# Two-layer graph network on one core: the MLP's products as column tiles between the edge groups, and first nodes read four at a time

## What is computed

```python
h = jnp.maximum(_layernorm(x), 0.0)
agg = segment_sum(edge_attr_64, dst) / jnp.maximum(counts, 1.0)[:, None]
x = x + (relu(concat([agg, h], 1) @ W1 + b1) @ W2 + b2)      # W1: 320 x 512, W2: 512 x 256
h = jnp.maximum(_layernorm(x), 0.0)
neigh = segment_sum(h[src], dst) / jnp.maximum(deg, 1.0)[:, None]
x = x + h @ w_self.T + b_self + neigh @ w_neigh.T
```

## Time and profile before

| | |
|---|---|
| median of 3 runs | 1132.64 us (1132.23 to 1134.74) |
| the profiled execution, its own time | 1135.44 us |
| its span (first to last instruction) | 1133.5 us |
| TensorE busy | 1072.6 us, 95% |
| VectorE busy | 787.8 us, 70% |
| ScalarE busy | 494.5 us, 44% |
| GpSimd busy | 521.7 us, 46% |
| mean granted TensorE clock | 0.985 of full speed |

### The profile page before, as it was taken

How to read it: one execution, slowest core, us unless ns; L and a number is a source line. 1 busy time by engine, 2 the same in 40 slices (tenths; PEclk the granted TensorE clock), 3 DMA queues, 4 the chain that set the end, 5 groups by cost and what they waited for, 6 DMA issues and landing times.

```text
span 1133.5 us, 29643 instructions
## 1 busy us (share of the span) xinstructions
PE 1072.6 (95%) x11380; PEld 792.0 (70%) x11380; DVE 787.8 (70%) x1849; ACT 494.5 (44%) x957; POOL 521.7 (46%) x502
## 2 busy tenths in 40 slices
PE   3689999999999999699999999999999999999998
PEld 2667777777777777467767777677677777776765
DVE  6778878887883667766766676766676767666762
ACT  4455646342212546444444444444444444444441
POOL 3011111110002664377576766774767676677520
PEclk9899999999999999699999999999999999999999
DMA  8776655555562221133233233332333333333210
GB/s 259 226 212 202 198 162 166 153 162 161 173 198 93 77 61 44 51 98 104 79 108 96 86 99 95 95 101 71 112 94 102 91 98 94 94 97 99 79 44 19
DMA packets 72618, 131.93 MB, mean 116 GB/s; under 512 B 12414, under 2 KB 32594, under 8 KB 72492
## 3 DMA queue, kind: packets, MB, share of 16 engines
q1 hardware_dynamic: 51820, 75.25, 21.7%
q0 software_dynamic: 20672, 55.00, 16.9%
HBM read 117.25 MB, written 12.95 MB: 115 GB/s over the span
## 4 chain that ended last, share of the span: by engine, by line
PE 87%; DVE 6%; DVEq 2%; ACT 2%; issue 2%; DMA 1%; ACTq 0%; SPq 0%
PE bank L1216 35%; PE couples L1209 10%; PE couples L1039 9%; PE bank L1235 7%; PE bank L984 7%; PE bank L996 6%; PE bank L978 2%; PE bank L1247 2%; PE bank L1227 2%; PE couples L1044 2%; PE couples L949 1%; DVE oreg L1647 1%; PE couples L984 1%; DVE oreg L1396 1%; DVEq L1511 1%
## 5 line engine op out<-in xcount | busy, mean ns | idle before, releaser
L1216 PE MATMUL bank<-hreg,areg 128*128 128x512 f16 x1862 | 457.0, 383 | 0.0
L629 POOL DMA_INDIRECT wide<-h_table,aggn x332 | 354.6, 1068 | 193.8 <-PE couples L1209 95.2
L847 ACT ACTIVATE areg<-couples 128x784 bf16<-128x784 f32 x304 | 250.3, 824 | 351.0 <-PE couples L1209 342.1
L1216 PEld LDWEIGHTS bank<-hreg,areg 128*128 128x128 bf16 x1862 | 240.4, 144 | 95.1 <-issue 1.6
L1647 DVE TENSOR_TENSOR hids<-iota,kreg 128x1024 bf16<-128x1024 f16 (+1 forms) x304 | 177.8, 626 | 110.0 <-PE couples L1209 108.9
L1647 DVE TENSOR_TENSOR oreg<-iota,kreg 128x1024 bf16<-128x1024 f16 (+1 forms) x304 | 177.7, 626 | 24.5 <-PE couples L1209 23.4
L1039 PEld LDWEIGHTS couples<-oreg,kreg 128*64 128x64 f32 x3232 | 117.2, 142 | 64.7 <-issue 63.6
L1039 PE MATMUL couples<-oreg,kreg 128*64 128x48 f32 x3232 | 138.5, 230 | 21.3 <-DVE oreg L1396 16.7
L597 POOL TENSOR_TENSOR xr<-xr,b2bc 128x512 f32 x25 | 33.9, 1356 | 221.0 <-ACT h0buf L719 221.0
L1396 DVE TENSOR_TENSOR oreg<-iota,wide 128x384 f32<-128x384 f32 x202 | 121.5, 602 | 4.4 <-issue 1.3
L996 PE MATMUL bank<-wide,hids 128*128 128x256 f32 x400 | 104.4, 398 | 0.0
(11 more groups left out here) (176 smaller groups left out, 1102.2 us busy)
## 6 DMA issues: line engine op xcount, KB each, us to landing
kreg<-in_edge_attr_dram SPq DMA_DIRECT2D x202, 256.0 KB, 2.8
h_table<-hreg SPq DMA_DIRECT2D x25, 256.0 KB, 2.2
xr<-in_x_dram SPq DMA_DIRECT2D x6, 1024.0 KB, 7.6
wide<-h_table,aggn POOLq DMA_INDIRECT x332
out_dram<-hbuf SPq DMA_DIRECT2D x38, 128.0 KB, 1.9
out_dram<-h0buf SPq DMA_DIRECT2D x10, 128.0 KB
wide<-in_L_gnn_W_dram SPq DMA_DIRECT2D x2, 512.0 KB, 8.5
hids<-h_table,aggn POOLq DMA_INDIRECT x64
```

What stands on the lines that cost most here:

```text
L629: pool.indirect_dma_start(near_rows(n % RING, w), None, table, bass.IndirectOffsetOnAxis(ap=nearsrc[:, k:k + 1], axis=0)).then_inc(s_rows[ ...
L847: act.activation(step.rearrange("p (a k) -> p a k", a=2), cpl[s % 2][:, :, 0:BC * KEYS], ACT.Copy).then_inc(s_adj, 1)
L1216: ins = pe.matmul(bank[4 + par], adj[:, par, :, h], htab[:, h, :], start=(h == 0), stop=(h == TN - 1))
```

## The change

- In the spans, `hidden` and `outer` are called with `beside=True`. Each product is then two, one for each half of its stationary columns (`halves_of`), written to the two halves of PSUM's partitions: column tiles of 64, as the groups' products are.
- `w1a` is no longer used as row tiles there: each piece multiplies all 128 rows of `w1a` (which holds the 64 rows of weights twice) by all 128 rows of `aggn[:, q, :]`. The half of `aggn` that DVE does not write for this q must be zero, so GpSimd clears `aggn` at the start, ahead of `acc`. The product with `w1a` for q = 1 moves into the piece of q = 1.
- PE's hardware loop over spans 2 to 5 is written out.
- The table `base` is clamped to 0..N-1 as it is written, and DVE reads the first nodes of groups g to g+3 in one load when g is a multiple of 4, without the range assertion; the three other groups use registers that are already filled.

```diff
+            pool.memset(aggn[:, :, :], 0.0)
             pool.memset(acc[:, :], 0.0).then_inc(s_const, 1)
...
+            def halves_of(beside):
+
+                return (slice(0, FE), slice(FE, P)) if beside else (slice(0, P),)
+
+            def hidden(i, k, b, q, own=0, beside=False):
...
-                    for e in qs:
-                        pe.matmul(hidden_bank(e, k, own)[:, b * NM:(b + 1) * NM], w1a[e * FE:(e + 1) * FE, cols],
-                                  aggn[e * FE:(e + 1) * FE, e, :], start=True, stop=False)
+                    if not beside:
+                        for e in qs:
+                            pe.matmul(hidden_bank(e, k, own)[:, b * NM:(b + 1) * NM], w1a[e * FE:(e + 1) * FE, at:at + P],
+                                      aggn[e * FE:(e + 1) * FE, e, :], start=True, stop=False)
...
+                if beside:
+
+                    for m in halves_of(beside):
+                        pe.matmul(into[m, :], w1a[:, at + m.start:at + m.stop], aggn[:, q, :], start=True, stop=False)
                 for h in range(DH):
-                    ins = pe.matmul(hidden_bank(q, k, own)[:, b * NM:(b + 1) * NM], w1b[:, h, cols],
-                                    h0T[:, bass.ds(2 * u, 2), h, :], start=False, stop=(h == DH - 1))
+                    for m in halves_of(beside):
+                        ins = pe.matmul(into[m, :], w1b[:, h, at + m.start:at + m.stop],
+                                        h0T[:, bass.ds(2 * u, 2), h, :], start=False, stop=(h == DH - 1))
...
-                    ins = pe.matmul(bank[6 + q][:, t * D:(t + 1) * D], hids[:, q, b, t * P:(t + 1) * P], w2s[:, b, :],
-                                    start=(b == 0), stop=(b == HB - 1))
+                    for m in halves_of(beside):
+                        ins = pe.matmul(bank[6 + q][m, t * D:(t + 1) * D], hids[:, q, b, t * P + m.start:t * P + m.stop],
+                                        w2s[:, b, :], start=(b == 0), stop=(b == HB - 1))
...
-                            part(i, *which)
+                            part(i, *which, beside=True)
...
-                loop(pe, lambda k: span(k, k - 1), 2, XPARTS)
+                for k in range(2, XPARTS):
+                    span(k, k - 1)
...
-            dve.tensor_copy(base[0:1, :], bank[6][0:1, 0:G]).then_inc(s_base, 1)
+            dve.tensor_scalar(base[0:1, :], bank[6][0:1, 0:G], 0.0, float(N - 1), ALU.max, ALU.min).then_inc(s_base, 1)
...
-                    return dve.value_load(base[0:1, bass.ds(SLOTS * i + q, 1)], min_val=0, max_val=N - 1)
+                    g = SLOTS * i + q
+                    if g % STARTS == 0:
+                        _, found = nc.values_load_multi_w_load_instructions(
+                            base[0:1, g:min(g + STARTS, G)], engines=[dve.engine], min_val=0, max_val=N - 1,
+                            skip_runtime_bounds_check_because="they are clamped as they are written")
+                        starts.update({g + n: v for n, v in enumerate(found)})
+                    return starts.pop(g)
```

More of the change, by code:

```diff
@@ L64, in gnn_kernel @@
     LAG = PARTS - 1
+    STARTS = 4
     H0 = 2, 2 + U
```

7 lines of the change are left out of this document (4 added, 3 removed).

## The result

The kernel before took 1133.67 us (median of 6 runs, 1132.23 to 1134.74), the changed one 1124.00 us (6 runs, 1119.82 to 1125.81). The ratio is 0.9902, 95% interval 0.9886 to 0.9918: 9.7 us less, where 27.4 were forecast. The time lies above the range.

A forecast was written before the change was run, and what follows sets the result against it. PE sets the pace from 72 to 343 us, DVE following closest. 29.4 - 1.5 + 1.0 - 0.5 - 1.0 = 27.4 us saved; 1132.64 - 27.4 = 1105.2, stated as 1106, range 1101 to 1117.

The forecast's parts named there:

- The mechanism on PE: Outer and hidden pieces, 72 to 343 us: tile-shape changes go, saving 17.9 and 11.5 us, together 29.4 of PE's 271.
- The rival of the exposed weight loads: PE's pieces: 560 instruction pairs each show 0.06 us of weight loading, 4.2 us slower, 1137; chance 0.05.
- that of the gaps that stay: PE's pieces: the 0.32 us gaps are not the tile's change and remain, 6.4 us slower, about 1139; chance 0.03.
- the charge for DVE: DVE's dense places in the spans: PE waits 0.3 us in each of five spans, 1.5 us lost.
- the dense place: DVE from the means at 208.04 to 219.97 us: 11.6 us busy against PE's 11.0 over the same eight groups.
- DVE's waits for PE: 72 to 343 us: without waits of 26.1 and 8.4 us DVE needs 236.5, PE 241.6; DVE fits, 5 us to spare.
- my second case, DVE takes over: Edge-group stretch: half of DVE's 34.5 us of waits stay as order; gain 17.5 us, time about 1116; chance 0.17.
- Edge rows: Edge loads behind three parts of x in the units: a wait of some 0.1 us and more each, charged 1.0 us.
- the stages after the last group, counted as shifted whole: Stages after 343 us: neither shortened nor lengthened by the change, only moved earlier.
- Reads: DVE's reads of first nodes, before 72 us: 27 reads fewer at 0.05 us each, 1.0 us gained.
- Start: Kernel start: clearing aggn ahead of acc holds DVE's index cast and shifts the whole start, 0.5 us lost.

The follow-up runs named there:

- the covered branch: Changed kernel with the first two hidden parts behind the spans moved ahead of the branch ending PE's group code: ratio 0.9871 to the kernel before.
- the best kernel: Changed kernel plus hidden pieces ahead of the branch, late x in four pieces, b2 added by TensorE for the seven units: 1109.81 us, 0.9762; again 1108.03, 0.9760.
- the kernel without column tiles: Kernel before with reads by four, covered branch, x in pieces and b2 on TensorE, loop over spans kept: 1126.78 us, 0.9919.

## Why the prediction was wrong

**The mechanism on PE and its size were right.** Outer piece and group went from 1.780 to 1.468 us: 0.31 us instead of 0.32, 56 x 0.312 = 17.5. A hidden pair went from 2.394 + 1.780 to 2 x 1.900 us: 0.37 instead of 0.41, 28 x 0.374 = 10.5. Together 28.0 us off PE, forecast 29.4. The rival of the exposed weight loads is out (1.47 and 1.90 us, halves 7 ns apart), as is that of the gaps that stay. The Trainium skill ("TensorE: Matmul & The Clock Gate", Part 3, The mechanism) has a list by which a weight load overlaps with matmuls in flight only where the rows differ, though the paragraph above it also lets a load into a background buffer go ahead. Here tiles with the same 128 rows follow each other at 0.216 us a pair, the time of streaming alone, so the measurement decides against the list's rule.

**The step that failed is the charge for DVE: 1.5 us, measured 12.3.** From the table: outer pieces stall for 89.7 - 79.3 = 10.4 us where the kernel before had 99.7 - 54 x 1.780 = 3.6, so 6.8; plain groups 29.1 - 23.6 = 5.5. I had found the dense place and priced it by its sum over eight groups (11.6 us of DVE against 11.0 of PE), at 0.3 us for each of five spans. PE does not wait for the sum but for single one-hots, three buffers ahead at most. In that very stretch of the kernel before DVE takes 3.3 us from one one-hot to the next (their ends, 211.31 and 214.57), where PE was to need 1.47:

```profile
211.35 0.22 DVE L1403 TENSOR_SCALAR deg<-areg 64x128 f32<-64x128 f32 x1
211.64 0.94 DVE L1405 RECIPROCAL deg<-deg 64x128 f32<-64x128 f32 x1
212.60 0.42 DVE L1392 TENSOR_TENSOR areg<-areg,couples 64x48 f32 x2
213.05 1.52 DVE L1396 TENSOR_TENSOR oreg<-iota,wide 128x384 f32<-128x384 f32 x1
```

Two things come together in it. One is GpSimd's addition of b2 (212.88 to 214.15): the one-hot took 1.52 us instead of 0.56, and I counted it without asking why. The trace of before had ten one-hots of over 0.8 us, 7.1 us of stretching in them, and a mean of 0.60 us for a one-hot. Leaving the addition out gives the stretch 6.6 us after (7.9 but for the lower clock) and 2.5 before, so 4.1 to 5.4 of the 12.3 us are the collisions'. The Trainium skill ("SBUF — State Buffer", SBUF: two separate sides) describes a port pair that VectorE and GpSimd hold one at a time for a whole instruction; the rows agree in the main (a one-hot begun at 207.89 under an addition that ends at 208.89 ends at 209.30, 0.41 us later, of the 0.56 that it takes alone). The other, the larger part, is what is left: DVE's own work, dense around the inverses and means, found by subtraction, since no run makes it shorter. Without the additions the tiles shorten the stretch by 266.5 - 249.4 = 17.1 us, still 10.9 less than they take off PE, of which 2.6 are waits for edge rows and 1.3 the lower clock.

The forecast also took DVE's waits for PE as time that DVE could give up, all but 5 us. In the stretch of the changed kernel it still waits 14.7 us for the groups' sums and 5.9 for hidden products, while PE waits for DVE: 20.6 of the 34.5 us stayed as a matter of order. That is what my second case, DVE takes over, said of half of them. It gave a gain of 17.5 us on PE; 28.0 - 12.3 = 15.7 is what it came to. I had it at 0.17, and no other charge beside it.

**Edge rows:** charged 1.0; PE waits 2.3 us for them where it waited 0.4, so 1.9 more, and the pieces with transposes are 2.4 us longer than with x in four pieces. Two of the late parts of x show such a wait. The mechanism was right.

**A second step that failed: the stages after the last group, counted as shifted whole.** 13.6 us became 17.2, 3.6 us lost. The first hidden product behind PE's branch comes 5.64 us after the last group instead of 4.20 (the branch itself takes 5.42 us instead of 4.20), and the 24 instructions from there take 2.14 us more at the lower clock, which fell over the idle time this time. The outer products ahead of the branch had not become shorter. Where the lower clock falls has no cause that the runs show: in the second execution of the changed kernel the place takes 15.8 us, without b2 13.8. Why the branch is longer stays open too. It takes 4.77 to 5.47 us in the six executions of kernels with column tiles that have nothing but the outer products ahead of it, 3.53 to 4.21 in the four without; writing out the loop alone left it at 4.21, though that kernel lost 3.2 us to an idle time further on. The loss goes with the covered branch (10.9 us).

**Reads:** +1.0 forecast, nothing measured. In the profiled execution 1.2 us are gained before the first hidden product, but column tiles with the old reads have that too (71.04 us), and the reads alone do not (73.74). That landmark goes with the clock: between 22 us and the first hidden product it was at the lower level for 10.2 us in the first of these, for 20.5 in the second, and for 13.7 in the kernel before and in the changed one. A load of four takes 343 ns against the 304 of the earlier trace rows, so the number of loads falls, but nothing shows that DVE's sequencer was waited for. **Start:** 0.5 us lost was forecast, and the first group comes at 22.41 instead of 21.94 us, with the cast's end (12.37 us: 11.91) as far behind:

```profile
6.29 6.08 DVE L1368 CAST hreg<-hreg 128x1024 f32<-128x1024 int32 x2 [6.29 <-DMA hreg<-in_dst_dram]
```

**The sum again:** 28.0 - 12.3 - 2.4 = 13.3 us in the stretch (13.0 by the landmarks; the last outer piece lies behind the last group), - 3.6 behind it, + 1.2 ahead of it: 11 us, and the spans differ by 10.7. That the 1.2 ahead of it come from the change is not shown, since that landmark moves with the clock.

What stays open: how much of DVE's own part a shorter inverse or mean would give back (moving the parts did not help), what makes the branch longer, the 5.7 us of PE's idle time in the best kernel, and whether moving b2 for all units would bring more.

## What to carry to other kernels

When PE sets the pace and another engine has 5 us to spare in 270, do not price that engine by its mean or by its sum over many steps: go step by step at the dense places, and ask for each whether it is shorter than what PE will need there. List the longest instances of the instruction that PE waits for, see what they collide with, and add those. Collisions that cost the slow kernel 2.5 us cost the fast one 6.6 or more. Where the second engine sets the pace at a place already (2.26 us behind group 15), a faster PE gains nothing there. At the end of a block look for a branch and for what lies ahead of it: here the branch was exposed in both kernels, and 5.2 us of products moved ahead of it closed the gap. And a change that is worth 1% may be worth 1.7% once its neighbours are mended: the whole change brought 9.7 us, and the column tiles 18.8 us after the branch, the edge rows and b2 had been seen to.

## What the runs showed of the hardware

A float16 product of 256 columns between row-tiled or whole products, put where the tile's shape changes, took 0.02 us: outer piece and group have a median of 1.80 us with it and 1.78 without in the kernel without column tiles. Among column tiles, where that gap is gone, it costs 0.08 us (1.551 against 1.468). The one-hots of VectorE (two inputs, 128x384) that took over 0.8 us instead of 0.56, 13 in the changed kernel and 10 in the one before, all began under a GpSimd addition (128x512) and ended 0.41 to 0.42 us behind it, the longest after 1.59 us. A branch out of an If block holds PE's queue for 3.3 to 5.5 us. In an idle time of 3.67 us behind it the clock went to the lower level and stayed there for 6.8 us, 5.8 of them over products; in the kernel before it went down while PE was busy. A load of four values to registers takes 343 ns, one of one value 304.
